# Value matmuls of two steps issued together in every second step, with eight slots for the exponentials

## The reference: attention plus a mixture of experts

```
scores = einsum('bihd,bjhd->bhij', q, k) * SCALE
attn = softmax(scores, axis=-1)
out = einsum('bhij,bjhd->bihd', attn, v).reshape(B, S, D) @ Wo + bo
x + attention(norm(x)) + experts(norm(x))
```

## Time and profile before

| | us |
|---|---|
| Median of 3 runs | 613.28 (606.53 to 615.7) |
| Span of the profiled execution, first to last instruction | 570.1 |
| Median less the span (launch and end) | 43.2 |
| PE busy | 493.9 (87%) |
| DVE busy | 418.9 (73%) |
| ACT busy | 311.2 (55%) |
| POOL busy | 136.7 (24%) |
| Mean granted clock of TensorE | 0.922 |

### The profile page before, as it was taken

How to read it: one execution, slowest core, us unless ns; L and a number is a source line. 1 busy time by engine, 2 the same in 40 slices (tenths; PEclk the granted TensorE clock), 3 DMA queues, 4 the chain that set the end, 5 groups by cost and what they waited for, 6 DMA issues and landing times.

```text
span 570.1 us, 9105 instructions
## 1 busy us (share of the span) xinstructions
PE 493.9 (87%) x2681; PEld 195.1 (34%) x2681; DVE 418.9 (73%) x821; ACT 311.2 (55%) x392; POOL 136.7 (24%) x195
## 2 busy tenths in 40 slices
PE   0695397867789998999899999989989998999995
PEld 0544231766742322233232233323222322232332
DVE  6579477567578887888688888868974887788412
ACT  1155100446565675667466676656663675567683
POOL 7317774222120000000000000000000002628682
PEclk9996655789999999999899999989995998999999
DMA  9206759268720011002000200200020011101111
GB/s 246 75 21 137 193 194 275 76 199 259 223 76 1 2 34 52 3 1 67 20 2 10 75 2 0 70 15 2 14 70 2 0 31 58 52 9 38 39 52 37
DMA packets 31068, 38.91 MB, mean 68 GB/s; under 512 B 5278, under 2 KB 27584, under 8 KB 29888
## 3 DMA queue, kind: packets, MB, share of 16 engines
q1 hardware_dynamic: 24368, 27.92, 17.6%
q0 software_dynamic: 3648, 9.44, 5.5%
q10 hardware_dynamic: 3024, 1.21, 0.8%
HBM read 25.78 MB, written 12.78 MB: 68 GB/s over the span
## 4 chain that ended last, share of the span: by engine, by line
PE 54%; DMA 18%; SPq 14%; DVE 6%; issue 5%; ACT 2%; DVEq 0%; ACTq 0%
PE banks L1039 17%; PE banks L1021 15%; PE banks L1076 14%; DMA q_rows<-q_parts 12%; SPq L309 4%; SPq L304 4%; SPq L316 3%; DMA w_blk<-in_wexp 3%; DVE half_max L791 2%; SPq L333 2%; DMA max_rows<-maxT 1%; SPq L318 1%; PE banks L1149 1%; PE banks L1133 1%; PE banks L948 1%
## 5 line engine op out<-in xcount | busy, mean ns | idle before, releaser
L791 DVE TENSOR_REDUCE half_max<-banks 128x1 f32<-128x512 f32 x512 | 323.2, 683 | 74.6 <-PE banks L1021 72.9
L603 ACT ACTIVATE probs<-banks 128x1024 f32<-128x1024 f32 x256 | 249.0, 1021 | 141.3 <-PE banks L1076 140.3
L1021 PE MATMUL banks<-k_rows,q_rows 72*128 72x512 bf16 x512 | 187.6, 408 | 11.7 <-DMA q_rows<-q_parts 7.5
L1076 PE MATMUL banks<-q_rows,k_rows 75*128 75x512 bf16 x512 | 154.5, 386 | 11.3 <-DMA q_rows<-q_parts 10.3
L1039 PE MATMUL banks<-probs,v_pad 128*32 128x512 f32 x1024 | 142.4, 629 | 0.6 <-ACT probs L603 0.6
L1021 PEld LDWEIGHTS banks<-k_rows,q_rows 72*128 72x128 bf16 x512 | 40.9, 99 | 167.9 <-DVE half_max L791 124.5
L1076 PEld LDWEIGHTS banks<-q_rows,k_rows 75*128 75x128 bf16 x512 | 49.1, 100 | 69.2 <-issue 18.8
L471 POOL TENSOR_TENSOR max_pad<-neg_max,zeros 128x16 bf16<-128x16 f32 x16 | 3.5, 220 | 281.1 <-DVE neg_max L796 278.1
L1039 PEld LDWEIGHTS banks<-probs,v_pad 128*32 128x32 f32 x1024 | 20.4, 109 | 55.0 <-issue 49.9
L450 POOL DMA_INDIRECT x_table<-xn,place_u x32 | 32.3, 1009 | 12.0 <-issue 12.0
L621 ACT ACTIVATE qf<-banks,w_blk 128x128 f32<-128x128 f32 x48 | 13.7, 368 | 29.3 <-PE banks L1140 29.3
(11 more groups left out here) (127 smaller groups left out, 332.5 us busy)
## 6 DMA issues: line engine op xcount, KB each, us to landing
w_blk<-in_wexp SPq DMA_DIRECT2D x48, 193.0 KB, 3.7
k_rows<-k_parts SPq DMA_DIRECT2D x24, 192.0 KB
q_rows<-q_parts SPq DMA_DIRECT2D x24, 192.0 KB
x_table<-zeros SPq DMA_DIRECT2D x1, 3072.0 KB, 12.4
moe_table<-probs POOLq DMA_DIRECT2D x12, 256.0 KB, 4.3
probs<-x_table POOLq DMA_DIRECT2D x8, 256.0 KB, 4.3
q_parts<-q SPq DMA_DIRECT2D x16, 96.0 KB, 2.0
k_parts<-k SPq DMA_DIRECT2D x16, 96.0 KB, 2.2
```

Source lines behind the costliest of these rows:

```text
L603: nc.scalar.activation(probs[:, n % 4, :, :], banks[:, 2 * pair:2 * pair + 2, :], ACT.Exp, scale=SCALE).then_inc(s_exp, 1)
L791: nc.vector.tensor_reduce(half_max[:, unit, row, half:half + 1], banks[:, 5 + job % RING, :], AX_X, ALU.max).then_inc(ring_free, 1)
L1021: pe.matmul(bank, q_rows[slot][0:PROD, j, q0:q0 + P], k_rows[slot][0:PROD, j, 512 * keys:512 * keys + 512], start=True, stop=True).then_in ...
L1076: mm = pe.matmul(banks[:, j, :], k_rows[slot][0:ROWS, j, P * kb:P * kb + P], q_rows[slot][0:ROWS, j, 512 * half:512 * half + 512], start=T ...
```

## The change

Three things change.

- `values` is no longer called in each step for the step before, but in every even step, for the two steps before: steps s-2 and s-1, one behind the other. Odd steps have no value matmuls. Behind the last step both remaining calls stand in a row.
- The exponentials get eight slots in place of four: the four of `probs`, three in the space of `q3` and one in that of `k3`, two tiles whose content has been stored to DRAM by then. ACT waits for those stores once, at the first turn.
- ACT's wait on `s_pv` moves from the values of two steps ago to those of four steps ago.

```diff
         probs = sb("probs", [P, 4, 2, 512])
+        parts_room = [a[:, :, :, :].rearrange("p c a n -> p (c a n)").bitcast(F32).rearrange("p (s k n) -> p s k n", s=3, k=2)
+                      for a in (q3, k3)]
+        prob_slots = [probs[:, i, :, :] for i in range(4)] + [parts_room[0][:, i, :, :] for i in range(3)] + [parts_room[1][:, 0, :, :]]
...
                         for i in range(2):
                             act.wait_ge(s_res_out[i], 16 * (GROUPS // 2))
 
-                    if s >= 2:
-                        act.wait_ge(s_pv, STEPS * t + s - 1)
-                    nc.scalar.activation(probs[:, n % 4, :, :], banks[:, 2 * pair:2 * pair + 2, :], ACT.Exp,
+                        for b in range(B):
+                            act.wait_ge(s_q3_out[b], 16 * 2 * NG)
+                            act.wait_ge(s_k3_out[b], 16 * 2 * NG)
+
+                    if s >= 4:
+                        act.wait_ge(s_pv, STEPS * t + s - 3)
+                    nc.scalar.activation(prob_slots[n % 8], banks[:, 2 * pair:2 * pair + 2, :], ACT.Exp,
                                          scale=SCALE).then_inc(s_exp, 1)
...
                 for j in range(HG):
                     mm = pe.matmul(banks[32 * j:32 * j + 32, 4, :], v_pad[:, slot, kb, j, :],
-                                   probs[:, (2 * s + j // 2) % 4, j % 2, :], start=(kb == 0), stop=(kb == KB - 1))
+                                   prob_slots[(2 * s + j // 2) % 8][:, j % 2, :], start=(kb == 0), stop=(kb == KB - 1))
...
-                if s > 0:
+                if s > 0 and s % 2 == 0:
+                    values(t, s - 2)
                     values(t, s - 1)
...
+            values(TURNS - 1, STEPS - 2)
             values(TURNS - 1, STEPS - 1)
```

## The result

The changed kernel takes 630.0 us (median of 4 runs, 628.2 to 641.1), the kernel before in the runs beside it 610.6 us. The ratio is 1.033 with an interval of 1.025 to 1.041: the change makes the kernel 3.3% slower. Single executions can take some per cent longer than the others of the same kernel (here the one of 641.1 us); the ratios and their intervals leave these out, the medians and ranges hold them. The prediction was 635, with 620 to 643 as its range.

The account below looks back on a forecast made before the run. PE was taken as the bound, DVE close behind; the paired order makes PE wait for the three-bank ring. Main part +18.4 and tail +3.5 give +21.9 us on 613.3: 635.2 us, 8-in-10 range 620 to 643.

Parts of the forecast that it names:

- The price of a double block: On PE, two value blocks in a row take 1.99 in place of 2.18 us, saving 0.18 per pair.
- The rival in which the third four matmuls pay the drain again: Rival, double block on PE: each pair 0.18 us longer, +33 us, 647 us; chance 0.08.
- The ring: Odd step: PE waits 0.41 us for DVE to free a bank at 2.37; two steps take 5.90, not 5.67.
- ACT's limit: Rival: even step's S1 waits for ACT until 3.14, pair 5.79, 624 us, chance 0.12; the forecast had ACT 0.11 short.
- The special pairs: Pairs with a turn of the values take 6.50 us, with a turn of the maxima 6.44, against 5.90 plain.
- Main part: The 116 steps with maximum jobs: eight steps take 24.74 in place of 23.44 us, +18.4 us in all.
- The tail: Last twelve steps: scores wait for ACT's exponential, pairs take 5.08 against 4.17; +3.5 us, ends 0 and 5.4.
- Half clock: Rival: more idle time on PE could lower its clock more often; left in the upper end, without its own chance.
- The base: Whole kernel: a span of 570.1 us and 43.2 around it make the median of 613.3.

Follow-up runs that it names:

- the two kernels with both engines relieved: Changed kernel, and single blocks with eight slots, both with DVE and ACT on 256 of 512 columns: plain pairs 5.43 and 5.67 us.
- Relieving DVE: Changed kernel with DVE reducing only 256 of 512 columns of each maximum job: plain pairs 5.76 us, ratio to before 0.999.
- relieving ACT: Changed kernel with ACT's exponentials on 256 of 512 columns, DVE unchanged: plain pairs 5.85 us; one run 628.5 us, beside 607.0 before.
- the first trace of before: Unchanged kernel before, the trace the prediction was read from: span 570.1 us.
- the kernel that pairs there alone: Kernel before with eight slots and double blocks only in the last twelve steps, after step 20 of the last turn: 574.3 us, beside 571.6.
- the kernel with slots alone: Kernel before with eight slots and the later s_pv wait, still one value block a step: ratio 1.005, plain pairs 5.67 us.
- early issue: Changed kernel with the double block and both scores of steps 20 and 36 ahead of the wait for rows: 591.6 us, ratio to before 1.035.
- split blocks: Changed kernel with the third maximum job put between the two value blocks of even steps: 619.8 us, plain pairs 6.00 us.
- the two early kernels: Values and both scores of steps 20 and 36 issued ahead of the wait: kernel before 554.3 us (0.979), changed kernel 591.6 us (1.035).
- the second trace of before: Unchanged kernel before, run again for a trace: 604.8 us, span 602.9 us, plain pairs 5.67 us.
- the tail was undone: Changed kernel with one value block a step again in the last twelve steps: 632.3 us, ratio to before 1.046.

## Why the prediction was right, and where it was off

**The price of a double block.** Predicted 1.99 with entry and exit in place of 2.18; from its start to the next matmul it takes 1.85 us (328.34 to 330.19), where 1.90 was expected. The third four matmuls do follow at once, 0.43 behind the second: their weights are loaded while the second run. PE's saving is thus 0.24 and not 0.18 us a pair, shown by the two kernels with both engines relieved. The rival in which the third four matmuls pay the drain again is out.

**The ring.** This was the step on which the sign hung, and it was right to 0.01 us: M3 of the odd step at 2.37. The pair is 5.85 and not 5.90, for the most part because of the shorter block. Relieving DVE moves the pair to 5.76 (ACT's limit), relieving ACT doesn't move it, relieving both gives 5.43. The ring as first limit and ACT's path just below it are shown, not only argued. In the prediction ACT was 0.11 short of binding; the two measured limits are 0.09 apart.

**The special pairs.** 6.50 and 6.44 were forecast; the trace has 6.55 or 6.68 with the turn of the values and 6.39 with that of the maxima. Eight steps: 24.74 forecast, 24.65 measured, with 1.17 us of idle time on PE where over 1.5 was forecast. Main part: +18.4 forecast; the pairs alone give 14.25 x (24.65 - 23.44) = 17.2 us over blocks 1 to 115, or 18 with every other turn of the values at 6.68. The +17.9 between the two spans agrees by luck: against the first trace of before, whose plain pairs are the same, it is +30.3 (391.7 - 361.4).

**The tail.** +3.5 forecast, +2.5 measured in the kernel that pairs there alone. A plain pair was to take 5.08 and takes 5.03, but I set it against 4.17, which holds only for steps without a projection or a turn of the values; the pairs that have one took 4.41 to 5.15 before. Those pieces that stand in odd steps fall wholly into the new wait (5.03), while those behind a double block, in even steps, are paid in full (6.01, 5.51). The changed kernel's tail, 37.9 us, is 6.0 longer than these 31.9. It has 5.9 us at half clock, and a wait of ACT and DVE for a queue that the profile doesn't name (1.9 us in the chain of waits; most likely a gather of POOL, which I didn't test). Neither comes with the change for certain: the kernel with slots alone had a tail of 39.5 us.

**Half clock.** I left it to the upper end and gave it no term, and this is where the prediction was off: its last sign of being wrong, "if the half-clock stretches grow", came true. The three traces with double blocks, DVE at full work and the stops for the rows have 54 to 60 us of half clock in the main part, and the one without those stops has 36, against 24 to 41 and 3 with single blocks. Where the stretches begin shows a part of the reason. After 408.86 the changed kernel is at half clock from 410.9 to 417.7:

```profile
408.86 0.39 PE L1028 MATMUL banks<-k_rows,q_rows 72*128 72x512 bf16 x1 [0.67 <-DVE half_max L798]
...
411.00:417.60 6.60, 6.60 (x24) 1.43 (x23) 2.37 (x6) 2.05 (x2) 0.00 (x0) 0.50 0.02 4
```

Nine stretches begin in its main part. Five stand at waits for the rows. The other four, some 24 of the 55 us, begin 1.3 to 2.0 us behind a stop of 0.67 to 1.18 us in which PE waits for DVE. Two of these four stops stand at the seam of the loop, ahead of the first maximum job of step 5 (or 37). The job count starts anew there, so `ring_slot` takes its other branch and waits until DVE has freed all three banks, and not only the bank of three jobs ago. The kernel before has the same stop, up to 0.73 us long, and none of its eight seams in two traces is followed by half clock within 2.5 us. Over all traces with DVE at full work, half clock begins within 2.5 us behind 10 of 16 seams in the four kernels with double blocks (behind all four with early issue, 31 of its 36 us), and behind 2 of 28 in the seven with single or split blocks. So a stop that both orders share brings half clock far more often in the paired rhythm. What in that rhythm does it stays open; I had no kernel that takes the wait at the seam away, and none that holds the pairs and changes only the spread of PE's idle time.

What it costs is less certain. By the main parts of the two early kernels it is 373.6 - 343.6 - 18 = 12 us for 32 us more at half clock, and PE's other new stops are in these 12 as well. That the time came out within 20 us of before, which the pairs and the tail alone make up (17 to 18 and 2.5), is luck in part. In the second trace of before one stretch of 17 us went by at half clock without double blocks, around a stop of 4.27 us that began with DVE and ACT waiting for a queue that the profile doesn't name. And the runs differ less than the traces: the mean granted clock was 0.883 to 0.894 in the three runs of the changed kernel behind the ratio, and 0.884 to 0.896 in six of the seven runs of before on the other chip of 610 us. On the chip where the tail was undone it was 0.877 to 0.886 with double blocks, beside 0.897 to 0.901 in the fastest four of before, and there the ratio was 1.046.

**The base.** The 43 us "around the span" were wrong. They didn't hurt, as the sum went on top of the median, but the terms were read from an execution 40 us shorter than the runs that they were set beside. Plain pairs took 5.67 in both.

## What to carry to other kernels

Before work is bundled on an engine to save switches, write down the schedule of one period with the buffers in it: a ring of three banks covers 3 x 0.60 = 1.8 us of its consumer, and a block of 1.85 us, plus 0.43 until the next job arrives, empties it; the jobs crowded into the rest of the period then run against the same ring. The saving was real (0.24 us a pair), and the ring (0.42) took more than that. The cheaper gain lay elsewhere: at a wait that stops an engine for a load, look which of the instructions behind it read that load, and issue the others first. What is left behind the wait then comes in a row: here four maximum jobs, of which the last had to wait 0.36 us for the ring.

## What the runs showed that I had not expected

- The kernel before takes 607 to 610 us on some chips and 572 to 577 on others. Between the two traces 17 us of it lie in the experts' part; steady steps are the same to 0.01 us.
- Issuing 1.95 us of work ahead of six stops for loads took 12 us off by the ratio (17 between the medians, 571.6 to 554.3), though the six stops themselves sum up to 10 us in either trace of before. The main parts of the traces, where half clock fell from 27 to 3 us, are 17.8 us apart.
- Rearranging a loop with the same work, and only 1.2 us of idle time in 24.65, went with 14 to 36 us more at half clock in the main parts of the traces, and in the changed kernel some 24 us of half clock stand behind stops of 0.67 to 1.18 us, two of them at the seam of the loop.
